# A decoder layer in float32: the same work in a new static order on all engines

## What is computed

```python
# x (32, 112, 256), ctx (32, 375, 256), 16 heads of 16
scores = einsum('bqhd,bkhd->bhqk', Q, K) * scale + alibi
x = layernorm(x + (softmax(scores, -1) @ V) @ Wo + bo)           # self-attention
sm = einsum('nlhd,nshd->nlhs', q, k) / sqrt(D)
sm = softmax(sm, axis=1)                                         # over the queries l
x = layernorm(x + einsum('nlhs,nshd->nlhd', sm, v) @ Wo + bo)    # cross-attention
x = layernorm(x + ffn(x))                                        # quantised, gated
```

## Time and profile before

| | |
|---|---|
| median of the three runs | 1372.14 us |
| the profiled execution | 1372.99 us |
| its span | 1371.2 us |
| TensorE busy | 1220.7 us, 89% |
| VectorE busy | 1140.3 us, 83% |
| ScalarE busy | 876.9 us, 64% |
| GpSimd busy | 343.0 us, 25% |

### The profile page before, as it was taken

One profiled execution on the slowest core, in us unless ns is written; L12 is line 12 of the kernel. 1 busy time (PEld: TensorE's weight loads), 2 busy tenths in 40 slices (PEclk: granted clock), 3 DMA queues, 4 the chain that ended last, 5 costly groups with the idle time before them and its releaser, 6 DMA issues. The chain is left out here.

```text
span 1371.2 us, 28241 instructions
## 1 busy us (share of the span) xinstructions
PE 1220.7 (89%) x8850; PEld 892.6 (65%) x8850; DVE 1140.3 (83%) x2358; ACT 876.9 (64%) x2290; POOL 343.0 (25%) x431
## 2 busy tenths in 40 slices
PE   1789999999999999999999999999976868759598
PEld 1466666666666666666666666666645757659598
DVE  6369999999999999999999999999973447868698
ACT  1366666666666666666666667666532449959695
POOL 0233432233343223333222334322210000000043
PEclk9899999999999999999999999999986989979799
DMA  5100001000000100000000000000000000000033
GB/s 161 38 20 19 19 19 31 21 18 21 18 18 18 32 18 18 21 18 18 22 29 18 18 21 18 19 26 13 4 8 4 0 0 1 0 0 1 17 101 97
DMA packets 35042, 33.07 MB, mean 24 GB/s; under 512 B 4148, under 2 KB 34604, under 8 KB 34988
## 3 DMA queue, kind: packets, MB, share of 16 engines
q1 hardware_dynamic: 32704, 31.50, 7.6%
q10 hardware_dynamic: 2284, 0.89, 0.3%
HBM read 25.04 MB, written 7.34 MB: 24 GB/s over the span
## 5 line engine op out<-in xcount | busy, mean ns | idle before, releaser
L561 ACT ACTIVATE Px<-score 125x896 f32<-125x896 f32 x192 | 176.2, 918 | 127.4 <-PE score L1080 66.1
L747 DVE TENSOR_REDUCE nmax_c<-score 125x8 f32<-125x896 f32 x192 | 208.4, 1086 | 6.0 <-PE score L1002 5.6
L729 DVE TENSOR_REDUCE Zc<-Px 125x8 f32<-125x896 f32 x192 | 206.8, 1077 | 7.9 <-ACT Px L561 4.4
L554 ACT ACTIVATE Ps<-score,nmax_s 112x112 f32<-112x112 f32 x512 | 173.6, 378 | 3.6 <-DVE nmax_s L754 3.6
L506 POOL TENSOR_TENSOR rstd<-vare,half 112x1 f32<-112x1 f32 x64 | 35.0, 548 | 474.5 <-DVE vare L839 474.5
L1080 PE MATMUL score<-sel,nmaxT 128*125 128x448 f32 x384 | 125.3, 407 | 1.8 <-ACT nmaxT L567 1.8
L554 ACT ACTIVATION_READ_ACCUMULATOR Ps<-score,nmax_s 112x1 f32 x512 | 118.8, 232 | 0.0
L1091 PE MATMUL outX<-Px,Vn 125*32 125x224 f32 x1536 | 113.4, 369 | 2.1 <-DVE Vn L740 2.1
L740 DVE TENSOR_TENSOR Vn<-Vx,rZc 125x128 f32<-125x128 f32 x192 | 112.8, 587 | 1.2
L567 ACT ACTIVATE nmaxT<-maxT 128x125 fp32r<-128x125 f32 x192 | 53.6, 279 | 89.6 <-PE maxT L1074 89.4
L1002 PE MATMUL score<-Qbd_hi,KxT_hi 64*125 64x448 f32 x384 | 90.4, 467 | 1.2 <-ACT Px L561 1.2
(11 more groups left out here) (245 smaller groups left out, 3482.3 us busy)
## 6 DMA issues: line engine op xcount, KB each, us to landing
ctx_in<-in_ctx SPq DMA_DIRECT2D x32, 375.0 KB
x_in<-in_x SPq DMA_DIRECT2D x32, 112.0 KB, 2.0
x_scratch<-x SPq DMA_DIRECT2D x32, 112.0 KB, 5.6
x2T_all<-x_scratch SPq DMA_DIRECT2D x32, 112.0 KB, 2.1
out<-x2T_all SPq DMA_DIRECT2D x32, 112.0 KB, 1.9
raw_w_up<-in_w_up SPq DMA_DIRECT2D x1, 768.0 KB, 5.6
raw_w_down<-in_w_down SPq DMA_DIRECT2D x1, 768.0 KB, 7.5
raw_w_gate<-in_w_gate SPq DMA_DIRECT2D x1, 768.0 KB, 9.6
```

The costliest lines, as they stand in the source:

```text
L554: ins = act.activation(Ps[:, g, :], score[slot][0:L, h // QUAD, (h % QUAD) * L:(h % QUAD + 1) * L], ACT.Exp, bias=nmax_s[:, g:g + 1], accu ...
L561: act.activation(Px[u % 2][:].rearrange("s (q h) l -> s q (h l)", q=2), score[SLOT_OF[f"C{u}"]][0:C, :, 0:QW], ACT.Exp).then_inc(exp_c, 1)
L729: dve.tensor_reduce(Zc[p][:], Px[p][:], AX.X, ALU.add).then_inc(z_c, 1)
L747: dve.tensor_reduce(nmax_c[u % 2][:, 0:OCT].rearrange("s (q h) -> s q h", q=2), score[SLOT_OF[f"C{u}"]][0:C, :, 0:QW].rearrange("s q (h l) ...
```

## The change

All five `step` functions of `attention` and the two tables of uses are written anew. No instruction that computes is added or removed, and sizes, buffers and semaphores are the same. The helpers that the steps call are unchanged.

- Work banks: all uses get a new bank or a new place. V0, V1 and K0, which a batch filled in one step before, now lie in two: K0 ends a step, V0 and V1 stand at the start of the next. Both banks have 11 uses (10 and 12 before).
- Score slots: the same units share the same slots in the same cyclic order, C4, C5, C1, C2 and C3, S1, C0, S0. Only the batch offsets change.
- TensorE: the scores of C1, C3 and C5 are now issued ahead of work on the unit before them (C1 before the transpose of C0's maxima, C3 before the shift of C2).
- VectorE, ScalarE: new orders to suit, with other batch offsets (an offset only says in which step a batch's item is counted).
- GpSimd: keys 0, queries 0, keys 1, queries 1, then the roots and the bias sums. Before: queries 0, a root, keys 0, keys 1, queries 1.
- SyncE: the context load first, then the store of x2, then the load of x.

```diff
 WORK_USES = (
-    (("Ks", 4), ("Qx", 2), ("PT1", 3), ("Qs", 4), ("ctxT0", 3), ("ctxT1", 3), ("AVs1", 3), ("Os", 3),
-     ("V1", 3), ("xT", 5)),
...
+    (("PT0", 5), ("V1", 4), ("PT1", 5), ("x1T", 4), ("Qx", 4), ("K1", 4), ("AVs0", 5), ("PT3", 5), ("AVs1", 5), ("Os", 5),
+     ("K0", 5)),
...
 SLOT_USES = (
-    (("C4", 1), ("C5", 1), ("C1", 2), ("C2", 2)),
-    (("S1", 3), ("C0", 2), ("S0", 4), ("C3", 2)),
+    (("C4", 3), ("C5", 3), ("C1", 4), ("C2", 4)),
+    (("C3", 3), ("S1", 5), ("C0", 4), ("S0", 6)),
 )
...
             def step(n0, n1, n2, n3, n4, n5, n6):
+                if n4:
+                    load_ctx(n4)
+                if n0:
+                    save_x2(n0)
                 if n5:
                     load_x(n5)
-                    load_ctx(n5)
-                if n0:
-                    save_x2(n0)
...
-                if n5:
-                    add_output_bias(n5)
-                if n4:
-                    diagonal_queries(n4, 0)
-                if n2:
-                    inverse_root(n2, 1)
-                if n6:
-                    diagonal_keys(n6, 0)
-                    diagonal_keys(n6, 1)
-                if n4:
-                    diagonal_queries(n4, 1)
...
+                if n4:
+                    diagonal_keys(n4, 0)
+                if n2:
+                    diagonal_queries(n2, 0)
+                if n4:
+                    diagonal_keys(n4, 1)
+                if n2:
+                    diagonal_queries(n2, 1)
+                if n0:
+                    inverse_root(n0, 1)
...
```

442 lines of the change are left out of this document (221 added, 221 removed).

## The result

The changed kernel takes 1334.96 us (median of four runs, 1332.38 to 1335.33), the kernel before 1372.16 us on the same chip (1371.88 to 1373.69). The ratio is 0.9723, with a 95% interval of 0.9706 to 0.9739. The profiled execution has a span of 1333.4 us (1371.2 before), which is 37.8 us less.

What follows compares the result with a forecast made beforehand. TensorE's own work of 28.95 us a step plus its wait for C0's maxima was taken as the bound. A wait of 1.65 us makes the period 30.6: 1373 + 21 - 4 = 1390 us, range 1343 to 1410.

Steps and rivals of the forecast that it cites:

- The place that decides: TensorE's transpose of C0's maxima, waiting 0.93 or 0.86 us a step for VectorE, delayed by a Vn of 1.66 us.
- Two kinds of delay: VectorE beside GpSimd's products: after idle time it gets in at the next boundary; deep in a row further products pass first.
- the first of the four ends: C4's Vn and the copy rZrep each get in at the next boundary: together 0.8 us late, less than the slack.
- The slack: VectorE's spare time before the transpose of C0's maxima: due at e + 6.0, work 4.6 us, slack 1.4 us.
- No order can make the period shorter: TensorE's own work for a batch, the same products in any order, takes about 28.95 us.
- the rival with the right mechanism: VectorE gets in at every boundary between GpSimd's products, so the 0.92 us wait goes: 1342 us, chance 0.20.
- What else could wait: TensorE waiting elsewhere: at C2's scores for Px, or at the transpose of C2's maxima, with some 0.4 us to spare.
- The drain: The last batch's cross units alone, with C1, C3 and C5 going ahead: -4 us, between -6 and -1.
- The count of 16 us: In the last batch, from C0's scores to C5's: about 16 us instead of 21.9.
- The filling: The first batches, with nearly the same items ahead of the first C0: 0, within 3 us.
- the case that came: VectorE gets in at every boundary between GpSimd's products, nothing replaces TensorE's 0.92 us wait: 1342 us, chance 0.20.
- the case with no delay: VectorE's requests let no further GpSimd product pass, so TensorE's wait at C0's maxima goes: 1342 us, chance 0.20.

Runs made afterwards that it cites:

- b_max_first: The kernel before, with VectorE making C0's maxima ahead of C4's Vn instead of behind it; 1346.87 us, ratio 0.9809.
- b_root_last: The kernel before, with GpSimd's second inverse root behind queries 1 instead of ahead of keys 0; 1348.27 us, ratio 0.9824.
- a_lock: The changed kernel with 42 test chains of eight GpSimd products ahead of its loop, VectorE asking at varied depths; 39 of 42 requests got in at the next boundary.
- a_lock2: The changed kernel with 32 other test chains ahead of its loop, varying the head of GpSimd's row (none, pow, small multiplication); requests took 0.67 to 6.31 us in the table and chains without head.
- a_x1b_late: The changed kernel, with x1b behind the first inverse root on GpSimd; 1329.84 us, ratio 0.9688.
- a_apart: The changed kernel, with three pairs of neighbouring items on TensorE taken apart; 1355.58 us.

## Why the prediction was wrong, step by step

- *The place that decides* was right: the transpose of C0's maxima, late by the Vn in front of them. Two single edits (b_max_first, b_root_last) remove the wait and bring 25.5 and 23.8 us, where the prediction priced it at 27.
- *"Two kinds of delay"* is the step that failed. The rule that a request deep in a row has to let products pass came from rows which all had the second root at their head. Ahead of the Qbd_hi at 499.69 GpSimd has

```profile
495.61 0.55 POOL L506 TENSOR_TENSOR rstd<-vare,half 112x1 f32<-112x1 f32 x1 [0.35 <-DVE vare L839]
496.12 0.93 POOL L485 TENSOR_TENSOR Kbd_hi<-Ks_hi,mask 128x448 fp32r<-128x448 f32 x1
```

and so in all 28 such steps. Depth and the root were never apart in that trace where products were left to pass, and the prediction took depth. The rule predicted 2.6 to 3.5 us of delay and a new wait of 1.65 us; 0.78 us of delay were measured, as in the first of the four ends (0.8), and no wait at this transpose. The change moves the root behind the products, which the text of the change says, and which the prediction passed over.
- *The slack*: e is 507.46 (the end of Qx's low part), the transpose was due at e + 6.0 and came at e + 5.62, VectorE's work was put at 4.6 + 0.8 and took 5.18. This arithmetic was good to 0.4 us.
- *"No order can make the period shorter"* than 28.95 us is the second step that failed. It is the term of the sum that was mis-sized ("the same set of products, so I keep 28.95 us"): the new order has 28.41 without waits, 0.54 less, which makes 16 us in 29 steps. Therefore even the rival with the right mechanism (1342) is 7 us too high.
- *What else could wait*: C2's scores and maxima did not. The second copy of rZrep, behind x1b, was not in the prediction, and it costs 0.12 us a step.
- *The drain*: -4 us was forecast, and C0 to C5 grew by 0.7. The count of 16 us left out that the order keeps the neighbouring batch's residual ahead of C2's maxima (1.6 us), and that TensorE's clock falls in this stretch (about 3 us). What else it missed stays open. The filling was right (0 within 3; -1.1 measured).
- *Chances*: the case that came had 0.20, on the ground that no row showed a Vn that got in deep in a row. That no row shows something was weak evidence, since no row could have shown it apart from the root. So the time fell below the range for two reasons: the case with no delay was held unlikely, and the shorter work of TensorE was in none of the cases.

## What to carry to other kernels

If a delay is explained by a rule read from a trace, list what all its cases have in common beside the property you picked; the one that the change removes is the one that matters. A small GpSimd instruction ahead of a row of large ones can cost VectorE the whole row, and putting it behind them cost nothing here. TensorE without idle time isn't yet at its limit: the order of its items is worth some 2% of a step here, where banks and buffers let two good neighbours stand side by side. And before a stretch at the end of a kernel is timed from another one, its granted clock is to be compared.

## What the runs showed of the hardware

- Between block-diagonal products of 0.89 us (start to start) VectorE's product of two SBUF operands or copy got in at the next boundary at seven depths (a_lock). Behind a pow of 0.55 us at the head of the row it is held until the last product, 7.22 us for a request in the first of eight; behind a multiplication of 0.19 us this was so for requests in the fourth and sixth product, and not in the second (a_lock2).
- VectorE holds GpSimd up in turn: in the chains the GpSimd product behind an entry of VectorE's product took 1.11 to 1.14 us instead of 0.93, and behind a copy it stayed at 0.93.
- With no idle time between them, the same TensorE item takes about a tenth of a microsecond more or less by what stands next to it: two `cross_values` 0.90 us together and 0.52 each apart, the transpose of the maxima 0.145 in the mean ahead of transposes and 0.257 ahead of `cross_values`. The change between products on 32 columns and on the whole array goes with it (0.28 us out of the 32 columns, 0.17 between two groups on them, a_x1b_late).
- TensorE's granted clock fell to its lower level (1.2 GHz) for 10.2 us of the last batch's cross units in the kernel after and 6.8 in the kernel before, after TensorE had stood idle for 0.36 to 1.19 us at a time between items. In a_apart, with the same idle times as in the kernel after up to there, it did not fall, and C0 to C5 took 19.4 us instead of 22.6.
